# A graph layer on one core: edge sums with destinations as rows, fixed ranges for pairs of batches, five slots of messages, and the mix by token and in place

## The reference

```python
xn  = layernorm(x)                                   # x: (6250, 256)
# 1. graph part
all_msg  = einsum('nf,rfo->rno', xn, weight)         # 16 relations, 256 -> 256
all_gate = einsum('nf,rf->rn', xn, gate_weight)
msg = all_msg[rel_type, src] * norm * sigmoid(all_gate[rel_type, src])
gnn = relu(segment_sum(msg, dst))
# 2. linear attention ("mix"): 8 heads of 64
q, k, v = split(xn @ w_qkv); k, v = inst_norm(k), inst_norm(v)   # per head
mix = (q @ (k.T @ v)) / n @ w_out + b_out
x = x + gnn + mix
# 3. mixture of experts, dense: 8 experts, top 2 weights
t = layernorm(x)
x = x + t + sum_e combine[:, e] * (gelu(t @ w1[e] + b1[e]) @ w2[e] + b2[e])
```

## Time and profile before

| | |
|---|---|
| median of 3 runs | 1849.27 us (1849.04 to 1849.43) |
| profiled execution, its own time | 1848.28 us |
| its span (first to last instruction) | 1846.5 us |
| mean granted clock of TensorE | 0.989 of full |
| PE / PEld / DVE / ACT / POOL busy | 1787.1 / 1600.8 / 1174.2 / 772.5 / 776.1 us |
| DMA | 296.06 MB, mean 160 GB/s |

### The profile page before, as it was taken

The page is one execution under the profiler, slowest core; times in us unless marked ns, Lnnn a source line. Parts: engine busy times, 40 slices in busy tenths (PEclk is TensorE's granted clock), DMA queues, the critical chain, the costliest instruction groups (busy, mean ns, idle before and its releaser), DMA issues.

```text
span 1846.5 us, 30572 instructions
## 1 busy us (share of the span) xinstructions
PE 1787.1 (97%) x11137; PEld 1600.8 (87%) x11137; DVE 1174.2 (64%) x3496; ACT 772.5 (42%) x1428; POOL 776.1 (42%) x812
## 2 busy tenths in 40 slices
PE   7999999999999799999699999999999999999998
PEld 5887888888888699998689999999999998999998
DVE  6555555444444666767558677677776867767764
ACT  5555666555554433332124333343343332433443
POOL 2000000000000366667776666666666666666700
PEclk8999999999999999999999999999999999999999
DMA  7665777755555574444433433433334343343400
GB/s 227 239 234 204 278 288 282 265 216 217 217 217 202 209 306 150 143 131 126 149 113 107 135 112 109 131 98 121 109 112 133 98 123 111 98 134 105 120 26 17
DMA packets 113914, 296.06 MB, mean 160 GB/s; under 512 B 18120, under 2 KB 73792, under 8 KB 104420
## 3 DMA queue, kind: packets, MB, share of 16 engines
q1 hardware_dynamic: 75236, 189.63, 27.6%
q0 software_dynamic: 38528, 104.46, 19.3%
HBM read 162.70 MB, written 131.32 MB: 159 GB/s over the span
## 4 chain that ended last, share of the span: by engine, by line
PE 92%; DVE 3%; POOL 2%; issue 1%; ACT 1%; DMA 1%; SPq 0%; DVEq 0%; ACTq 0%
PE bank L51 23%; PE bank L53 22%; PE bank L52 22%; PE bank L1346 18%; PE bank L1335 2%; POOL plain L590 2%; PE bank L1411 1%; PE bank L1239 1%; PE bank L1451 1%; DMA plain<-messages,idxT 1%; PE bank L1214 1%; PE bank L1401 1%; PE bank L1392 1%; DVE parts L620 0%; DVE plain L958 0%
## 5 line engine op out<-in xcount | busy, mean ns | idle before, releaser
L590 POOL DMA_INDIRECT plain<-messages,idxT x784 | 765.3, 976 | 966.9 <-issue 825.5
L51 PE MATMUL bank<-parts 128*128 128x512 f32 (+2 forms) x2232 | 812.7, 364 | 9.9 <-DVE plain L991 5.0
L53 PE MATMUL bank<-parts 128*128 128x512 f32 (+2 forms) x2232 | 785.9, 352 | 0.0
L52 PE MATMUL bank<-parts 128*128 128x512 f32 (+2 forms) x2232 | 784.7, 352 | 0.0
L51 PEld LDWEIGHTS bank<-parts 128*128 128x128 f32 x2232 | 425.4, 191 | 59.8 <-DVE plain L991 6.0
L53 PEld LDWEIGHTS bank<-parts 128*128 128x128 f32 x2232 | 423.6, 190 | 55.2
L52 PEld LDWEIGHTS bank<-parts 128*128 128x128 f32 x2232 | 425.4, 191 | 46.8
L1346 PE MATMUL bank<-plain 128*128 128x128 f32 x3136 | 389.6, 279 | 23.1 <-DMA plain<-messages,idxT 19.4
L1346 PEld LDWEIGHTS bank<-plain 128*128 128x128 f32 x3136 | 374.8, 195 | 29.8 <-DMA plain<-messages,idxT 21.9
L1165 ACT ACTIVATE plain<-bank,small 128x512 f32<-128x512 f32 (+1 forms) x208 | 135.3, 663 | 372.2 <-PE bank L53 368.9
L663 DVE TENSOR_SCALAR plain<-bank,plain 128x256 f32<-128x256 f32 x392 | 171.0, 478 | 164.5 <-PE bank L53 110.9
(11 more groups left out here) (150 smaller groups left out, 987.6 us busy)
## 6 DMA issues: line engine op xcount, KB each, us to landing
messages<-plain SPq DMA_DIRECT2D x49, 2048.0 KB, 7.0
parts<-xnT_scratch SPq DMA_DIRECT2D x20, 1024.0 KB, 5.3
xnT_scratch<-parts SPq DMA_DIRECT2D x98, 128.0 KB, 3.3
plain<-messages,idxT POOLq DMA_INDIRECT x784
w_parts<-parts SPq DMA_DIRECT2D x32, 256.0 KB, 2.4
parts<-w_parts SPq DMA_DIRECT2D x4, 2048.0 KB, 20.6
plain<-in_x SPq DMA_DIRECT2D x48, 128.0 KB, 7.0
plain<-in_x SPq DMA_DIRECT2D x10, 512.0 KB, 4.3
```

The source lines that it names most:

```text
L51: e.matmul(out, left(0), right(0), start=start, stop=False)
L52: e.matmul(out, left(0), right(1), start=False, stop=False)
L53: return e.matmul(out, left(1), right(0), start=False, stop=stop)
L590: e.indirect_dma_start(msg[:, b % SLOTS, j, :], None, table_rows, bass.IndirectOffsetOnAxis(idxT[:, j, b:b + 1], 0)).then_inc(s_gather[b % ...
```

## The change

Five edits that hang together:

1. The edge sum swaps its operands: the one-hot is stationary, the message rows (256 columns) are moving. The result has destinations as rows and all features as columns. `agg` is now [128, 49, 256], nodes as rows.
2. Batches go in pairs with a fixed range: pair i (batches 2i-1 and 2i; batch 0 alone) covers the 128 nodes from `64*(i-1)`. Both batches are summed in one bank, and DVE adds once a pair, in one piece where the range is one tile, or in two pieces of 64 rows. `offT` is the destination modulo 128. Register loads of bases go. `enough(g)` becomes the first batch whose range lies behind the group.
3. Five slots of messages in place of four.
4. The mix is by token: xn is stationary, `mix_p` is moving, tokens come out as rows; the bias is a product of a row of ones with `b_out`. DVE adds max(agg, 0) and the mix into `agg` and then x, in place. `mix_back`, its transposes, ACT's copy and `acc` are gone. `mix` has two steps a group of two tiles each (at `ready` 0 and 3). xn and x of two tiles are loaded for each (`load_mix`, `load_residual`), each through one buffer. `norm_tile` moves from DVE to ACT.
5. Memory is laid out anew for this; `w_out` and `wqT` are loaded after the last `dots`, and the first xn for the mix after them.

```diff
-SLOTS, HOTS = 4, 3
+SLOTS, HOTS, LOOK = 5, 3, 2
+    STEP = 2 * BATCH * N // E                                   # 64
+    PAIR_OF = [(b + 1) // 2 for b in range(BATCHES)]
+    ROW0 = [STEP * max(0, i - 1) for i in range(PAIR_OF[-1] + 1)]
     def enough(g):
-        return BATCHES if START[g + 1] == TILES else -(-START[g + 1] * P * E // N // BATCH) + LAG
+        return min([b for b in range(BATCHES) if ROW0[PAIR_OF[b]] >= START[g + 1] * P] + [BATCHES])
...
             def sum_batch(b):
                 e.wait_ge(s_gather[b % SLOTS], 16 * CHUNKS * (b // SLOTS + 1))
                 e.wait_ge(s_onehot, b + 1)
-                if b >= 2:
-                    e.wait_ge(s_add_batch, b - 1)
-                for h in range(KH):
-                    for j in range(CHUNKS):
-                        m = e.matmul(bank[b % 2][:, h * P:(h + 1) * P], msg[:, b % SLOTS, j, h * P:(h + 1) * P],
-                                     onehot[:, b % HOTS, j, :], start=j == 0, stop=j == CHUNKS - 1)
+                i = PAIR_OF[b]
+                first, last = b == 0 or b % 2 == 1, b % 2 == 0 or b == BATCHES - 1
+                if first and i >= 2:
+                    e.wait_ge(s_add_pair, i - 1)
+                for j in range(CHUNKS):
+                    m = e.matmul(bank[i % 2][:, 0:D], onehot[:, b % HOTS, j, :], msg[:, b % SLOTS, j, :],
+                                 start=first and j == 0, stop=last and j == CHUNKS - 1)
...
+            def add_pair(i):
+                ...
+                t, row = divmod(ROW0[i], P)
+                spans = [(0, P, t)] if row == 0 else [(row, P, t), (0, row, t + 1)]
+                for r0, r1, t_ in spans:
+                    if t_ < TILES:
+                        m = e.tensor_tensor(agg[r0:r1, t_, :], agg[r0:r1, t_, :], bank[i % 2][r0:r1, 0:D], ALU.add)
...
-            def mix(g, h):
+            def mix(g, p):
...
+                for k in range(2 * p, min(2 * p + 2, SIZE[g])):
+                    o = bank[3][:, (k % 2) * D:(k % 2 + 1) * D]
+                    for i in range(2):
+                        e.matmul(o, one_p[0:1, :], bout_p[0:1, i, :], start=i == 0, stop=False)
+                    for q in range(KH):
+                        m = three(e, o, lambda i: xnT_g[:, i, q, (k % 2) * P:(k % 2 + 1) * P], lambda i: mix_p[:, i, q, :],
+                                  False, q == KH - 1)
...
+            def add_mix(g, p):
+                ...
+                e.scalar_tensor_tensor(rows_, rows_, 0.0, bank[3][:, 0:(k1 - k0) * D].rearrange("p (k o) -> p k o", o=D),
+                                       ALU.max, ALU.add).then_inc(s_misc, 1)
+                ...
+                e.tensor_tensor(rows_, rows_, x_in[:, 0:k1 - k0, :], ALU.add).then_inc(s_x_added, 1)
...
+            def load_mix(m):                                     # SP
+                if m:
+                    e.wait_ge(s_mix_sum, m)
+                else:
+                    e.wait_ge(s_dots, TILES)
+                    e.wait_ge(s_squares, 2 * TILES)
+                    e.wait_ge(s_head_vars, 3 * TILES)
+                ...
+            def load_residual(m):                                # SP
+                if m:
+                    e.wait_ge(s_x_added, m)
+                else:
+                    e.wait_ge(s_mix_low, 1)
+                ...
...
-                e.tensor_scalar(x3[:, k % 2, :], acc[:, g % 2, k, :], mvB[:, k, 0:1], sdB[:, 2, k:k + 1],
-                                ALU.subtract, ALU.mult).then_inc(s_x3, 1)              # DVE
+                e.activation(x3[:, k % 2, :], agg[:, START[g] + k, :], ACT.Identity, bias=sdB[:, 3, k:k + 1],
+                             scale=sdB[:, 2, k:k + 1]).then_inc(s_x3, 1)               # ACT
```

More of the change, by code:

```diff
@@ L18 @@
 BATCH = CHUNKS * P
-WINDOW = P
 GROUP = 4
@@ L209, in gps_layer @@
         if s[0] == "batch":
-            n_batch = s[1] + 1
-            mixes_done[s[1]] = n_mix
+            n_pair = PAIR_OF[s[1] + 1] if s[1] + 1 < BATCHES else len(ROW0)
         if s[0] == "mix":
[L213 to L218, removed]
+            mix_use[s] = len(mix_use)
+            last_pair[s] = n_pair
     turns_before = {}
@@ L278, in gps_layer @@
         route_p = parts.carve(KH, 2, X)
-        parts.at = piece_at
-        piece_p = parts.carve(2, 2, BANK)
+        bout_p = parts.carve(2, D)
+        one_p = parts.carve(P)
+        with nc.sbuf_tensor("piece_parts", [P, 2, 2, BANK], F32R) as piece_p:
+            pass
+        with nc.sbuf_tensor("squares", [P, VK], F32) as sq_t:
+            pass
+        sq = sq_t[:, :]
+        mixes = Arena(sb("mix_parts", [P, 2048], F32R), 2048)
+        mix_p = mixes.carve(2, KH, D)
+        xnT_g = mixes.carve(2, KH, 2 * P)
         parts.at = 0
@@ L320, in gps_layer @@
[L320 to L324, removed]
+        ones1 = plain.carve(P)[0:1]
+        hs = rest.carve(6, 2 * INNER // HEAD)
+        rest_at = rest.at
+        v_s = rest.carve(2, INNER)
+        k_s = rest.carve(2, INNER)
+        rest.at = rest_at
+        bd = rest.carve(PAIRS, P)
+        fold = rest.carve(PAIRS, D)
+        wout_s = rest.carve(PAIRS, D)
@@ L910, in turn_norm @@
                 for k in ks:
-                    m = e.tensor_tensor(acc[:, s, k, :], acc[:, s, k, :], x3[:, k % 2, :], ALU.add)
+                    m = e.tensor_tensor(agg[:, START[g] + k, :], agg[:, START[g] + k, :], x3[:, k % 2, :], ALU.add)
                 m.then_inc(s_acc, 1)
-                if i == 0:
-                    for k in range(2, SIZE[g]):
-                        norm_tile(g, k)
             def route(g):
@@ L1035, in vector_program @@
                 elif step == "mix":
-                    relu_add(*a)
-                elif step == "mix_back":
-                    add_back((step, *a))
-                    if a[1] == KH - 1:
+                    add_mix(*a)
+                    if a[1] == (1 if SIZE[a[0]] > 2 else 0):
                         x2_stats(a[0])
@@ L1157, in turn_norm @@
                        bank[3][:, :].rearrange("p (h n) -> p h n", h=KH)[:, :, 0:k * P]).then_inc(s_x3T_high, 1)
+                if i == 0:
+                    for k in range(2, SIZE[g]):
+                        norm_tile(g, k)
             def gelu(g, x_):
@@ L1185, in scalar_program @@
                     e.copy(mix_p[:, 0, :, :], bank[2][:, :].rearrange("p (h o) -> p h o", h=KH)).then_inc(s_mix_high, 1)
-                elif step == "mix":
-                    mix_copy(*a)
                 elif step == "norm":
@@ L1190, in scalar_program @@
                     e.activation(sdB[:, 1, 0:SIZE[a[0]]], sdB[:, 0, 0:SIZE[a[0]]], ACT.Sqrt).then_inc(s_x2_sqrt, 1)
+                    for k in range(min(2, SIZE[a[0]])):
+                        norm_tile(a[0], k)
                 elif step == "turn_norm":
```

344 lines of the change are left out of this document (151 added, 193 removed).

## The result

The changed kernel takes 1852.51 us (median of 20 runs, 1851.41 to 1854.27). The kernel before took 1848.81 us beside it (20 runs, 1847.2 to 1851.26). The ratio is 1.002, 95% interval 1.0014 to 1.0026: it is 3.7 us slower, and the whole interval lies above 1. The profiled execution has a span of 1849.6 us against 1846.5.

The account below looks back on a forecast made before the run. It took PE's matmul stream to bound most of the kernel, and gathers 870 to 940. Terms -10.6 - 5.0 - 1.4 + 2.7 + 16.9 + 0.4 = +3.0 on 1849.27 gave 1852 us, range 1835 to 1860.

Parts of the forecast that it names:

- The batch sums: Edge sums on PE: four 256-column matmuls for eight of 128 save 0.059 us in each of 180 batches, -10.6 us.
- Five slots: Gather-bound stretch 870 to 940: one more message slot lets POOL get one batch further ahead, -5.0 us.
- The late wait: Single gather wait between 1400 and 1600, taken away by the fifth slot and the shorter `enough`, -1.4 us.
- The mix by token: Mix on PE: 256-column matmuls replace 512-column ones and transposes, 0.06 us more a tile over 45 tiles, +2.7 us.
- The bias with one row: Mix on PE: going from 128 rows to one and back costs 0.375 us in each of 45 tiles, +16.9 us.
- The start: Kernel start: two ACT copies and a DVE subtraction put ahead of most weights delay the first message tile, +0.4 us.
- Off PE: Changed work on DVE, ACT and SP's queue, apart from the start, was claimed to cost PE nothing.
- What would show it: Trace signs: 8-record batch about 1.9 us, weight-load idle before the bias 49 times, gather waits from 19.4 to about 14.
- Rival C: 870 to 940 bound by the chain of loads behind the last `dots`, so 5.0 us not gained: 1857 us, chance 0.13.
- Rival D: Edge sums on PE: the swapped operands gain nothing, +10.6, 1863 us, chance 0.05.

Follow-up runs that it names:

- experiment 7: Kernel before with only the edge sum's operands swapped (output wrong): ratios 0.9935 and 0.9924 to the kernel before, both on the slower chip.
- experiment 6: Changed kernel with four message slots in place of five: 1859.05 us, ratio 1.0055 to the kernel before; on the slower chip 0.9834.
- experiment 1: Changed kernel with the mix's bias matmuls over 128 rows (127 of zeros) in place of one: 1835.82 us, ratio 0.9929 to the kernel before.
- experiment 4: Changed kernel with the one-row bias matmuls of both tiles of a pair issued together first: ratios 0.9854 and 0.9838 to the kernel before, slower chip only.
- experiment 5: Changed kernel with the mix's bias matmuls over 64 rows (63 of zeros) in place of one: 1990.24 us, ratio 0.9893 to the kernel before, slower chip.

## Why the prediction was right

The time (1852 for 1852.5), the sign and the mechanism came out. That the sum hits to half a microsecond is luck in part: the errors by stretch, up to 0.8 us, cancel. Step by step:

- **The batch sums**, -10.6. Right in size: 0.060 us a batch for the swap (0.059 forecast). A tile of the K/V stage fell by 0.078 to 0.080, not 0.06. The other 0.02 lies in the fourth to seventh full matmul behind a batch, whose starts are 1 to 9 ns closer to their forerunners than before; the swap alone doesn't do this (experiment 7), and which edit does stays open. It is why the second row of the table has -3.2 and not -2.4.
- **Five slots**, -5.0. Measured 5.65 between the two kernels and 5.2 for the slot alone. The 6.5 us of experiment 6 hold another 1.6 at the lower clock, which the prediction had not counted; before and after the change the last dense batch runs at full speed (2.05 us in the earlier trace rows, 1.99), so the change did not get it. They are also not all the slot's: 1.2 us of the difference of the two traces stand ahead of the second edge sum, where experiment 1, with five slots, is late by 2.0 too.
- **The late wait**, -1.4: gone, but it goes with four slots too (experiment 6).
- **The mix by token**, +2.7: its pitch is the forecast 0.12 (1022.38 to 1022.50). A group of the expert stage takes 75.4 us from one L1455 to the next (1013.06 to 1088.45), 74.4 to 74.5 before (1019.98 to 1094.43 at L1451). Between most groups it is 0.94 to 0.96 more. The terms say 4 x 0.38 + 4 x 0.06 - 12 x 0.06 = +1.04.
- **The bias with one row**, +16.9: 45 x 0.380 = 17.1 in the trace. Taking it away gave 17.2 in the traces and 16.7 in the time (experiment 1). The reading of 1.68 against 1.30 us in the earlier trace rows, from another line with 16 rows, was enough to find it; experiment 4 shows that the trip is paid once per change, and experiment 5 that 64 rows pay it too. The rule of the Trainium skill (TensorEngine Tiling (Array Packing), Key Properties) that a change of tiling mode drains TensorE fits, if 1, 16 and 64 rows count as other modes than 128, and 97 and 99 do not. The runs show the price of a change, not that it is a drain. The one from TensorE: Matmul & The Clock Gate (Why this matters for your kernels), that a single matmul with K=32 takes the time of K=128, fits the pitch within a block from its second matmul on, 0.12, and not the change; 32 rows themselves were not run.
- **The start**, +0.4: the trace has +1.0, in another place. The first edge sum came 0.37 earlier (643.77 for 644.14), but the work behind it ran at the lower clock for longer. The batch took 3.75 us for 3.42, and the next `dots` began 1.0 later than before. Both kernels stand 3.7 us just before. The granted clock from the edge sum to 649.80, before and after:

```profile
644.14:649.80 5.66, 5.66 (x27) 5.23 (x28) 2.32 (x9) 0.00 (x0) 1.66 (x2) 0.74 1.03 437
```

```profile
643.77:649.80 6.03, 6.03 (x15) 4.79 (x15) 2.32 (x9) 0.00 (x0) 1.70 (x2) 0.51 1.01 429
```

  At 0.51 it is at the lower level nearly all the time, before only for half of it. Why it rose later was not tried, and it may have little to do with the change: from the first edge sum to the second it takes 8.30 us here, 6.91 before, and 7.08 and 7.06 in experiments 1 and 6, whose first sum stands at 646.95 and 646.20. One trace of each kernel can't tell 0.4 from 1.0 here.
- **Off PE**, nothing: not quite. In the last group, where nothing stands between, the norm on ACT (at 1785.27 and 1791.53) goes ahead of the cast that DVE L645 needs, and that makes the first 256-column matmuls of an expert late: 1.2 us in the row of costs by form.

```profile
L48 PE MATMUL bank<-parts 128*128 128x256 f32 x784 | 235.7, 301 | 6.7 <-DVE agg L993 5.4 <-DVE parts L645 1.2
```

  So PE waits 6.7 us before this line, where it waited 5.0 before. The prediction had named more than 5.0 us of such waits as a sign that it is wrong; by that sign this step failed, at a price of 1.2 to 1.7 us that it had put at nothing. The last stretch then adds up to -138 x 0.060 + 2.7 + 17.1 - 1.4 + 1.2 = +11.3, where +10.9 was measured; the other 0.4 stays open.
- **What would show it.** The batch of 8 records takes 1.89 us (1.9 forecast). The gather waits went from 19.4 to 12.4 (14). One sign was named wrongly: the weight loads' idle before the bias line was to be seen 49 times.

```profile
PEld bank L1393 <- issue: 4.7, 14, 0.4
```

  It lists 14 of them: those behind an edge sum or behind a matmul of 384 or 512 columns. The other 35 trips cost the same 0.38 us but show in no wait, only in the distance of the starts. Who had looked for the waits alone would have put the price at 4.7 us.

Rival C (the loads bind 870 to 940) is out: no line of `fold` or `mix` waits for a load there, and the 5.65 us were gained. Rival D is out by experiment 7.

So one detail paid back more than the whole change gained. Without the round trips it takes 1835.8, and with the bias on DVE 1826.0: the other edits, with the bias on DVE, are worth 22.0 us (1847.99 - 1825.97), and the way in which the bias came in costs some 26.

## What to carry to other kernels

Where TensorE is the bound, look at each place where the number of rows (the contraction) of consecutive matmuls changes. A row of ones times a bias looks like 0.24 us for its two matmuls and cost 0.62 here, 0.38 of it for the trip there and back. Pad such an operand with zeros to 128 rows, collect the narrow matmuls of several tiles in one block, or give the work to an engine with room; and find such prices by the distance between starts, since the view of waits showed only 14 of 49 of them.

## What the runs showed of the hardware

- Leaving 128 rows and coming back costs TensorE 0.37 to 0.38 us at the full clock, the same for 1, 16 and 64 rows, and nothing that the starts show for 97 and 99. Each of the two changes costs 0.19: 0.09 before the first matmul of the new kind and 0.10 before its second.
- At equal streamed columns, an f32 matmul of 256 columns (two records, 0.216 apart) beats two of 128 (four records, 0.1117 apart) by 0.015 us, 0.060 for a batch of four chunks.
- In a row of batches with a wait each, the granted clock changes from batch to batch (1.00 and 0.62), and a batch takes from 1.99 to 3.8 us. Where the last batch was hit, what stands behind it came 1.6 us later.
- One chip took 6 to 9% longer for the three kernels timed on both, with the extra behind 603 us, and put the changed kernel with four slots ahead of the kernel before (0.9834), where elsewhere it is behind (1.0055). A ratio to a shared reference did not cancel this.
